# A fused state-space and two-MLP block on one core: the second half of `w2` moved into the next tile's program, a new table of slots, ten more products on GpSimd

## The reference

```
x = x + block_A(layernorm(x))
x = x + block_B(layernorm(x))

block_A(u): h = u + mamba(rmsnorm(u) * n1);  return h + silu(xn @ gate.T) * (xn @ up.T) @ down.T,  xn = rmsnorm(h) * n2
mamba(u):   z, x, B, C, dt_raw = split(u @ in_proj.T);  dt = softplus(dt_raw @ dt_w.T + dt_b)
            state = exp(dt * A) * state + (dt * x) * B        (over the 1024 tokens, 256 channels x 32 states)
            y = sum over states of state * C;  y = (y + x * D) * silu(z);  return y @ out_proj.T
block_B(x): hidden = silu(x @ W1.T) * (x @ W3.T);  return hadamard(hidden) @ W2.T       (1024 wide)
```

## Time and profile before

| | us |
|---|---|
| median of 3 runs | 1129.17 (1128.63 to 1129.44) |
| the profiled execution | 1129.54 |
| its span, first to last instruction | 1127.5 |
| before scan 0 of tile 0 | 39.0 |
| tiles 0 to 7, from scan 0 to scan 0 | 109.0, 129.3, 126.0, 127.1, 126.0, 127.2, 126.0, 123.5 |
| after the last scan | 94.4 |
| busy: PE, DVE, ACT, POOL | 1017.4, 1006.2, 629.5, 868.9 |

### The profile page before, as it was taken

The page is one execution under the profiler, slowest core; times in us unless marked ns, Lnnn a source line. Parts: engine busy times, 40 slices in busy tenths (PEclk is TensorE's granted clock), DMA queues, the critical chain, the costliest instruction groups (busy, mean ns, idle before and its releaser), DMA issues.

```text
span 1127.5 us, 13622 instructions
## 1 busy us (share of the span) xinstructions
PE 1017.4 (90%) x3816; PEld 525.6 (47%) x3816; DVE 1006.2 (89%) x1133; ACT 629.5 (56%) x1267; POOL 868.9 (77%) x444
## 2 busy tenths in 40 slices
PE   3486689899999999999999999999999989898998
PEld 1222134446454554436453554446453543446777
DVE  4599999999999999999999999999999999997342
ACT  4455675548755675548655675548655554443220
POOL 2589898788988798888988798888988888785100
PEclk9686699999999999999999999999999999999999
DMA  6998899997999899997989798997999798870000
GB/s 229 220 210 203 195 234 246 234 222 183 234 215 223 176 231 197 226 206 191 236 205 219 176 233 201 225 205 187 234 209 208 174 228 182 191 162 19 1 1 19
DMA packets 124602, 213.93 MB, mean 190 GB/s; under 512 B 18608, under 2 KB 27760, under 8 KB 124400
## 3 DMA queue, kind: packets, MB, share of 16 engines
q1 hardware_dynamic: 122800, 209.36, 82.7%
q0 software_dynamic: 1008, 3.67, 0.9%
q10 hardware_dynamic: 720, 0.04, 0.0%
HBM read 185.99 MB, written 12.06 MB: 176 GB/s over the span
## 4 chain that ended last, share of the span: by engine, by line
PE 66%; DVE 14%; issue 8%; ACT 7%; DMA 3%; SPq 1%; POOL 1%; DVEq 0%; POOLq 0%; ACTq 0%
PE p_r L581 17%; PE p_r L570 10%; DVE h_s L1110 9%; PE p_r L587 9%; PE p_y L536 7%; PE p_dt L525 6%; PE p_r L576 5%; PE p_r L556 3%; DVE bt_s L1092 3%; ACT p_dt L742 2%; PE p_dt L681 2%; PE p_r L681 2%; ACT tok L791 2%; DMA bt_s<-dx_rows 2%; PE p_r L691 1%
## 5 line engine op out<-in xcount | busy, mean ns | idle before, releaser
L1374 POOL TENSOR_TENSOR h_s<-h_s,c_s 128x1024 f32<-128x1024 f32 x255 | 556.0, 2183 | 125.2 <-DVE h_s L1110 123.0
L742 ACT ACTIVATE p_dt<-p_dt,an_s 128x512 f32<-128x512 f32 x372 | 241.4, 660 | 247.6 <-PE p_dt L525 247.4
L1110 DVE TENSOR_TENSOR_SCAN h_s<-p_dt,carry,bt_s 128x512 f32<-128x512 f32 x256 | 319.2, 1270 | 6.6 <-ACT p_dt L742 6.4
L1110 DVE TENSOR_TENSOR_SCAN h_s<-p_dt,bt_s 128x512 f32<-128x512 f32 x256 | 302.6, 1211 | 13.1 <-ACT p_dt L742 13.0
L525 PE MATMUL p_dt<-kdt,pick_s 128*128 128x512 f32 x372 | 231.4, 635 | 65.9 <-DVE h_s L1110 53.5
L1349 POOL TENSOR_TENSOR bt_s<-bt_s,b_s 128x1024 f32<-128x1024 f32 x101 | 238.9, 2365 | 17.7 <-DMA bt_s<-dx_rows 12.7
L581 PE MATMUL p_r<-nT,w_s 128*128 128x512 f32 x448 | 204.7, 597 | 0.7
L1092 DVE TENSOR_TENSOR bt_s<-bt_s,p_b 128x1024 f32<-128x1024 f32 x155 | 186.3, 1202 | 9.0 <-DMA bt_s<-dx_rows 9.0
L525 PEld LDWEIGHTS p_dt<-kdt,pick_s 128*128 128x128 f32 x372 | 72.6, 198 | 200.5 <-DVE h_s L1110 131.5
L570 PE MATMUL p_r<-nT,gu_s 128*128 128x512 f32 x308 | 143.5, 599 | 3.8 <-ACT nT L944 3.8
L536 PE MATMUL p_y<-h_s,ysel_s 128*32 128x512 f32 x1024 | 143.9, 636 | 1.8 <-POOL h_s L1374 1.8
(11 more groups left out here) (152 smaller groups left out, 931.5 us busy)
## 6 DMA issues: line engine op xcount, KB each, us to landing
bt_s<-dx_rows SPq DMA_DIRECT2D x512, 256.0 KB, 5.9
dtr_s<-dt_rows SPq DMA_DIRECT2D x224, 128.0 KB, 6.5
dtr_s<-dt_rows SPq DMA_DIRECT2D x112, 64.0 KB, 6.0
...
```

The lines of the kernel that those rows point to most:

```text
L742: A(p_dt[DT_BANK[u]][:, :], dt_in, ACT.Exp, scale=an_s[:, c:c + 1]).then_inc(a_dA, 1)
L1110: V.tensor_tensor_scan(h_s[:, u % 8, 1:T + 1], p_dt[DT_BANK[u]][:, :], bt_s[:, u % 16, :], carry[:, u:u + 1] if par else 0.0, ALU.mult, AL ...
L1374: G.tensor_tensor(h_s[:, two, 0:T], h_s[:, two, 1:T + 1], c_s[:, h, :].unsqueeze(1).broadcast_to([P, 2, T]), ALU.mult)\
```

## The change

The second part of `w2` leaves the body in which the first part runs. As stage `("v2", 0)` its 16 products stand in slot 1 of the *next* body, behind `c1` and ahead of `uT`; VectorE's addition follows in slot 2, GpSimd's store in slot 4. Since body `i` works on tile `i-1` in its last stages, `v2` in body `i` belongs to tile `i-2`, and there is none in bodies 0 and 1. In the last body the second part for tile 6 is run by `last_second_half` in slot 62 (TensorE) and 63 (VectorE), in a bank of its own choice (`SPARE`). `c1` now waits only for the first addition of the tile before.

`PLAN` is written anew: most parts keep their order and shift by a slot or two. The first part of `w2` stands in slots 57 to 61, `dtp1` in 57 (its softplus in ScalarE's slot 58, low half of `dt` on VectorE in slot 61), `z` in 7 to 8 and 9, `hT` in 11, `dtp0` and the last `gate` in 25. `POOL_FIRST` has 9 products, `POOL_ODD` 15 and `POOL_EVEN` 14. Some small steps of ScalarE, SyncE and GpSimd get other slots.

```diff
-POOL_FIRST = [0, 3, 6, 9, 13, 16, 19, 22, 26, 29]
-POOL_ODD = [0, 3, 5, 9, 11, 13, 16, 19, 21, 24, 25, 27, 29]
-POOL_EVEN = [0, 3, 5, 9, 11, 13, 16, 19, 21, 24, 25, 27, 29]
+POOL_FIRST = [0, 3, 6, 9, 14, 16, 19, 22, 26]
+POOL_ODD = [0, 5, 6, 9, 10, 11, 13, 16, 19, 20, 22, 23, 24, 27, 29]
+POOL_EVEN = [0, 1, 3, 7, 8, 11, 13, 16, 18, 21, 23, 24, 25, 29]
...
 PLAN = [
-    ("c1", 0, 2, 1, 1), ("uT", 0, 4, 1, 1), ("uT", 1, 4, 1, 1), ("xb", 0, 2, 4, 5), ("out", 0, 4, 5, 5),
-    ("out", 1, 4, 5, 6), ("z", 0, 2, 9, 9), ("z", 1, 2, 9, 9), ("dtr", 0, 2, 10, 13), ("hT", 0, 4, 12, 12),
...
-    ("w3", 6, 2, 50, 50), ("w1", 7, 2, 51, 52), ("dtp1", 0, 1, 53, 53), ("w3", 7, 2, 53, 53),
-    ("w2", 0, 16, 55, 57), ("w2", 1, 16, 59, 61)
+    ("c1", 0, 2, 1, 1), ("v2", 0, 16, 1, 1), ("uT", 0, 4, 1, 1), ("uT", 1, 4, 2, 2), ("xb", 0, 2, 4, 5),
+    ("out", 0, 4, 5, 5), ("out", 1, 4, 5, 6), ("z", 0, 2, 7, 8), ("z", 1, 2, 9, 9), ("dtr", 0, 2, 10, 11),
+    ("hT", 0, 4, 11, 11), ("hT", 1, 4, 11, 11), ("gate", 0, 2, 12, 12), ("gate", 1, 2, 13, 14),
+    ("up", 0, 2, 13, 13), ("gate", 2, 2, 17, 17), ("up", 1, 2, 17, 18), ("up", 2, 2, 18, 19),
+    ("gate", 3, 2, 19, 19), ("gate", 4, 2, 19, 23), ("up", 3, 2, 21, 23), ("up", 4, 2, 22, 25),
+    ("dtp0", 0, 1, 25, 25), ("gate", 5, 2, 25, 25), ("down", 0, 12, 27, 28), ("down", 1, 12, 30, 31),
+    ("c0", 0, 2, 31, 32), ("xT", 0, 4, 35, 36), ("xT", 1, 4, 36, 36), ("w1", 0, 2, 36, 36), ("w1", 1, 2, 37, 37),
...
+    ("w3", 6, 2, 51, 52), ("w1", 6, 2, 51, 52), ("w1", 7, 2, 52, 52), ("w3", 7, 2, 55, 55), ("w2", 0, 16, 57, 61),
+    ("dtp1", 0, 1, 57, 57)
 ]
...
-XL_SLOT = 60
+XL_SLOT = 62
...
-SUM_SLOT = 51
-W2_SLOT = 15
+SUM_SLOT = 48
+W2_SLOT = 13
...
-KEPT_SLOT = 5
-DT_STEP = -3
+KEPT_SLOT = 10
+DT_STEP = 0
...
+SPARE = (BANK["w2", 0] + 1) % RING
...
+                    if i == LAST and u == max(60, ENDS["w2", 0] + 1):
+                        last_second_half()
...
+            def last_second_half():
...
+                ps = ring[SPARE]
+                for j in range(16):
+                    s, f = 2 + j // 8, j % 8
+                    ins = nc.tensor.matmul(ps[:, D * (j // 8):D * (j // 8) + D], hd_s[:, f, P * s:P * s + P], w2_s[:, f, :],
+                                           start=(f == 0), stop=(f == HB - 1))
+                ins.then_inc(mm["w2"], 1)
...
+            def add_second_half(t, par, ps):
+
+                dve.wait_ge(mm["w2"], t * 2 + 2)
+                dve.wait_ge(a_xn, t + 1)
+                V.tensor_tensor(res[:, par, 2:4, :], ps[:, :].rearrange("p (s d) -> p s d", d=D), res[:, par, 2:4, :],
+                                ALU.add).then_inc(v_o, 1)
...
+                        if i >= 2 and u == ENDS["v2", 0] + 1:
+                            add_second_half(i - 2, par, ring[BANK["v2", 0]])
+                        if i == LAST and u == U - 1:
+                            add_second_half(pt, other, ring[SPARE])
...
+                    if i >= 2 and u == ENDS["v2", 0] + 3:
+                        store(i - 2, par)
```

More of the change, by code:

```diff
@@ L90 @@
 PLAN = [
[5 rows of a table removed]
-    ("gate", 5, 2, 24, 24), ("down", 0, 12, 24, 28), ("down", 1, 12, 29, 31), ("c0", 0, 2, 31, 35),
[5 rows of a table removed]
+    ("c1", 0, 2, 1, 1), ("v2", 0, 16, 1, 1), ("uT", 0, 4, 1, 1), ("uT", 1, 4, 2, 2), ("xb", 0, 2, 4, 5),
+    ("out", 0, 4, 5, 5), ("out", 1, 4, 5, 6), ("z", 0, 2, 7, 8), ("z", 1, 2, 9, 9), ("dtr", 0, 2, 10, 11),
[3 rows of a table added]
+    ("dtp0", 0, 1, 25, 25), ("gate", 5, 2, 25, 25), ("down", 0, 12, 27, 28), ("down", 1, 12, 30, 31),
[5 rows of a table added]
 ]
@@ L484, in _ @@
                      "up": (v_mh, GB + 1), "down": (v_x1, 2), "xT": (a_xT, 2), "w1": (v_fa, HB), "w3": (v_hd, HB),
-                     "w2": (v_o, 2)}
+                     "w2": (v_o, 2), "v2": (v_o, 2)}
             def done(stage, k, tile):
                 s, per = freed[stage]
-                k = {"dtp1": 1}.get(stage, k)
+                k = {"dtp1": 1, "v2": 1}.get(stage, k)
                 if (stage, k) == ("gate", GB):
@@ L511, in bank_free @@
                 if from_tile(i, 2):
-                    stage = [PLAN[p] for p in uses if PLAN[p][0] not in PRE | MID][-1][0]
-                    s, per = freed[stage]
-                    pe.wait_ge(s, (i - 1) * per)
+                    stage, k = [PLAN[p] for p in uses if PLAN[p][0] not in PRE | MID | {"v2"}][-1][:2]
+                    done(stage, k, i - 2)
             def spread(i, u):
@@ L583, in dense @@
                 else:
-                    s, f = 2 * k + j // 8, j % 8
-                    if k == 0:
+                    s, f = (2 if stage == "v2" else 0) + j // 8, j % 8
+                    if stage == "w2":
                         pe.wait_ge(v_hd, t * 8 + f + 1)
@@ L589, in dense @@
                 if j == n - 1:
-                    ins.then_inc(mm[stage[:3] if stage[:3] == "dtp" else stage], 1)
+                    ins.then_inc(mm[{"dtp0": "dtp", "dtp1": "dtp", "v2": "w2"}.get(stage, stage)], 1)
             def transform_w2(k):
@@ L620, in on @@
                 def on(stage):
-                    return pre if stage in PRE else units if stage in MID else post
+                    return pre if stage in PRE else units if stage in MID else i >= 2 if stage == "v2" else post
                 for u in range(U):
@@ L1219, in body @@
                                         V.bn_aggr(mv[:, 1, s, :], bn[:, 1, s, :]).then_inc(v_mv2, 1)
-                            if u == min(ENDS["w2", k] + 2, U - 1):
-                                dve.wait_ge(mm["w2"], pt * 2 + k + 1)
+                            if k == 0 and u == min(ENDS["w2", 0] + 2, U - 1):
+                                dve.wait_ge(mm["w2"], pt * 2 + 1)
                                 dve.wait_ge(a_xn, pt + 1)
@@ L1350, in drive, with store @@
                                 b_s[:, h, :].unsqueeze(1).broadcast_to([P, 2, T]), ALU.mult).then_inc(g_bt, 1)
+            def store(t, par):
+                pool.wait_ge(v_o, t * 2 + 2)
+                pool.dma_start(rows(out_t, t), res[:, par]).then_inc(l_out, 16)
             def body(i, par, pre, units, post):
@@ L1405, in body @@
                                 .then_inc(g_r3, 1)
-                if post:
-                    pool.wait_ge(v_o, pt * 2 + 2)
-                    pool.dma_start(rows(out_t, pt), res[:, other]).then_inc(l_out, 16)
+                if i == LAST:
+                    pool.wait_ge(a_xl, i + 1)
+                    store(pt, other)
             def tail():
```

5 lines of the change are left out of this document (4 added, 1 removed), and 8 rows, old and new, of the table PLAN.

## The result

| | before | after |
|---|---|---|
| median of 4 runs each | 1129.11 us (1128.63 to 1129.44) | 1152.64 us (1151.07 to 1155.09) |
| ratio | | 1.0209, 95% interval 1.0192 to 1.0226 |
| profiled execution: span | 1127.5 us | 1153.1 us |

What follows compares the result with a forecast made beforehand. The prediction took VectorE's queue, its work plus waits, to end each tile. Tile gains and losses plus +3.1 us after the last scan summed to -2.4 us on a profiled 1129.54; with the median 0.4 lower, 1126.8, range 1117.5 to 1136.5.

Steps and rivals of the forecast that it cites:

- The boundary: Tile start: VectorE's addition in slot 2 waits for `v2` on TensorE, 4.4 us in even and 3.1 in odd tiles.
- the third rival: Slots 58 to 62: the softplus wait only moves, seven tiles lose some 1.3 us, +9, 1135.8 us; chance 0.12.
- The second rival: Odd tiles: GpSimd's backlog from consecutive drive products delays sums and scans, +12, 1138.8 us; chance 0.14.
- The -1.12: Even tiles: one drive product fewer on VectorE, worth -1.12 us.
- the gain of 0.5 at `down`: Slot 32, even tiles: `down`'s second part stands a slot closer, saving 0.5 of 0.9 us of wait.
- the 0.2 for a bank: Slot 41, even tiles: one bank is waited for, +0.2 us.
- the 0.8 for a tanh: Slot 26, even tiles: the tanh wait goes because TensorE is further ahead by then, 0.8 us gained.
- the 1.2 us set for debts: Slots 0 to 14, even tiles: TensorE's remaining work debt and GpSimd's later `rs` for `hT`, +1.2 us.
- The products' 2.24 us: Odd tiles: two drive products fewer on VectorE, worth -2.24 us.
- not -3.8: Tile 1, without `v2`: fewer drive products, one addition fewer and shorter waits, together -3.8 us.
- I cost this at nothing: Slot 63: SyncE, held by GpSimd's later `dx` product, issues transfers late; no cost, up to 3 us a tile without cover.
- The first rival: Whole kernel: boundary debt is paid by the waits it replaces; ten drives fewer save 11.2 us, 1118.0 us; chance 0.14.

Runs made afterwards that it cites:

- The run that mended the two waits: Changed kernel with the slots of `dtr` to `w3` (10 to 53, the middle slots) and `w2`'s transform as in the kernel before: 1142.95 us (1.0108).
- The exchange: Changed kernel with SyncE issuing run 3 of tile 1 ahead of the wait for the `dx` product in slot 63 of tile 0: 1149.65 us (1.0171).
- the move alone: Kernel before with only `w2`'s second half put in slot 1 of the next tile, addition behind it, store three slots later: 1164.43 us (1.0294).

## Why the prediction was wrong, by its steps

**The boundary.** The count was right: 4.4 and 3.1 us of wait were forecast at the addition in slot 2, 4.1 and 3.2 came. The waits in slots 52 to 57 and 63 went as said, and the softplus was hidden, which refutes the third rival: in the changed kernel VectorE waits 0.3 us for exponentials in tile 4. The second rival is refuted for the steady tiles: GpSimd waits 13.3 us for scans in tile 5, more than the 12 that I had forecast at most, and no wait of TensorE for GpSimd there reaches 1 us.

**Even tiles +2.4, not +0.3.** One step gave work to the wrong tile: I took one product from each even tile and two from each odd one, and between the scans 0 it is none and three. The -1.12 was not there to win in an even tile, where VectorE is busy for 120.9 us in tile 4 in both kernels. This moves 1.1 us from the even tiles to the odd ones and leaves the forecast's sum as it is. Then two waits were forecast wrongly: the gain of 0.5 at `down` in slot 32 was a loss of 0.7 (1.6 us against 0.9), and the 0.2 for a bank in slot 41 was 1.0, in slot 43. Of the 0.8 for a tanh 0.4 came. Against that, the 1.2 us set for debts shows in no wait of slots 3 to 14. Together this is the missing 2 us, to some tenths. The run that mended the two waits still gained nothing in even tiles, because the lists had a price behind them that no term held: with the new lists alone the even tile grew by 2.1 us, since they put products ahead of two `rs`. I had written that one of them comes one drive later and put it into the 1.2 us of debt. With the middle slots and the even list as before, the even tile is 126.8, +0.8.

**Odd tiles +1.3, not -0.4.** Three products went, not two, and VectorE's busy time fell by 3.0 us in tile 5. But its waits rose by 4.1 us where I had 1.8: beside the 3.2 at the boundary, `down` waits 1.3 instead of 0.3, slot 43 1.3 instead of nothing, and a tanh 0.6, the size of the debt. The products' 2.24 us were also taken as if they came through whole. Beside the middle slots of before the odd list is worth 0.5 for two products (128.8 to 128.3), beside the new ones, with all lists, 1.1 for three, and in the kernel before -0.5, though it took 2.4 us off VectorE's busy time there. VectorE's queue isn't all that ends an odd tile.

**Tile 1 +9.4, not -3.8, the largest miss, 13.2 of the 28.0 us.** The step was "I cost this at nothing, since VectorE's wait in slot 2 holds the scans back by as much". The text named the hold, the queue behind it and a price without cover of 3 us. But tile 1 has no `v2` and so never had the cover. The exchange shows 11.9 us against the profiled execution of the changed kernel and 6.9 against the shortest with the same tile 1; with it tile 1 is 2.5 us shorter than before, near the forecast. The failure is a cover that was argued for the tiles with `v2` and applied to all, in the tile in which the transfer engines are full. Whether it holds in the others no run tests.

**Tile 7 +4.8, not +1.0.** The addition waits 3.2 us as forecast. The rest is the middle slots (2.6 of it, by the run that sets them back) and, as far as can be told, a granted clock of 0.97 against 0.99. Tile 0 (-2.8, forecast -2.7) and the stretch behind the last scan (+3.9, forecast +3.1) were right.

**The granted clock was in no step.** I took the length of TensorE's instructions from a trace in which its clock was full in all steady tiles, and the sum had no term for it. The Trainium skill (TensorE: Matmul & The Clock Gate, Part 1) says that idleness puts TensorE at half its clock, and that for modelling the cost of the ramp is under 1% of a typical span. The first agrees with the rows above. By the second the clock could be left out of a sum of this kind, though the page gives it for the ramp, and in the move alone the clock falls again at each tile. The runs show at least 10.2 us of 1164.4, 0.9%, in the move alone. That is within the page's figure and more than four times what a measurement of this kernel can tell.

The first rival, the rule to relieve VectorE, is refuted by the run with the lists alone: 1136.2 us where ten products less should have given 1118.
